# The 71 routed slots of a mixture-of-experts kernel, written out instead of looped over pairs

## The reference, cut to what matters

```python
x = L0_attn_x                                # (4, 1024, 512): 4096 tokens of 512 features
xn = _layernorm(x)
s = _L0_attn_ref(xn, ...)                    # layernorm, q k v, causal softmax, o_proj, + residual
# _L0_ffn_ref, E = 8 experts, K = 2 per token, H = 352:
gates = softmax(xf @ router_w.T)
topv, topi = lax.top_k(gates, K)             # masked gates, divided by their sum
def step(acc, p):
    y = _silu(xf @ wg_e) * (xf @ wu_e) @ wd_e
    return (acc + y * g_e[:, None], None)
routed, _ = lax.scan(step, zeros_like(xf), (wg, wu, wd, masked.T))
shared = _silu(xf @ sg) * (xf @ su) @ sd
g = _silu(routed + shared)
return x + s * g
```

## Time and profile before

| | |
|---|---|
| median of 3 executions | 1150.11 us |
| profiled execution, its own time | 1149.77 us |
| its span, first to last instruction | 1148.0 us |
| PE busy | 1131.4 us (99%) |
| DVE, ACT, POOL busy | 572.4, 473.5, 423.6 us |
| mean granted clock of TensorE | 0.997 of full speed |

### The profile page before, as it was taken

One profiled execution on the slowest core, in us unless ns is written; L12 is line 12 of the kernel. 1 busy time (PEld: TensorE's weight loads), 2 busy tenths in 40 slices (PEclk: granted clock), 3 DMA queues, 4 the chain that ended last, 5 costly groups with the idle time before them and its releaser, 6 DMA issues. The chain is left out here.

```text
span 1148.0 us, 21220 instructions
## 1 busy us (share of the span) xinstructions
PE 1131.4 (99%) x6598; PEld 627.4 (55%) x6599; DVE 572.4 (50%) x1236; ACT 473.5 (41%) x859; POOL 423.6 (37%) x656
## 2 busy tenths in 40 slices
PE   8999999999999999999999999999999999999997
PEld 5555555555556555555555555554454454444454
DVE  6876666677469331222111221112477377367467
ACT  5544344435332232333223232234654645555643
POOL 1333233332400222222222222212755754764763
PEclk9999999999999999999999999999999999999999
DMA  9899999989533599999997777776876777766364
GB/s 277 221 238 215 239 239 224 220 212 239 137 76 67 131 191 206 208 202 203 204 190 197 178 184 175 172 177 152 168 184 171 166 160 189 152 161 184 109 156 120
DMA packets 365003, 209.31 MB, mean 182 GB/s; under 512 B 304308, under 2 KB 314816, under 8 KB 364936
## 3 DMA queue, kind: packets, MB, share of 16 engines
q1 hardware_dynamic: 354104, 172.76, 64.7%
q0 software_dynamic: 10800, 35.69, 12.6%
q10 hardware_dynamic: 32, 0.02, 0.0%
HBM read 89.44 MB, written 46.01 MB: 118 GB/s over the span
## 5 line engine op out<-in xcount | busy, mean ns | idle before, releaser
L706 PE MATMUL pair<-arena 128*128 (+2 forms) x3240 | 506.2, 313 | 2.9 <-DMA arena<-arena 2.7
L706 PEld LDWEIGHTS pair<-arena 128*128 128x128 f16 x3240 | 316.0, 98 | 185.6 <-DMA arena<-arena 3.2
L1647 DVE SCALAR_TENSOR_TENSOR arena<-pair,slot_unit,arena 128x352 f32<-128x352 f32 x71 | 41.5, 584 | 269.1 <-ACT arena L1537 212.6
L713 PE MATMUL bank<-arena 128*128 x639 | 149.3, 379 | 0.0
L1537 ACT ACTIVATE arena<-pair,slot_unit 128x352 f32<-128x352 f32 x71 | 39.3, 554 | 205.4 <-PE pair L706 178.5
L1251 POOL COPY arena<-token_of 128x1 uint32 (+1 forms) x71 | 12.9, 181 | 265.2 <-issue 103.1
L1941 PE MATMUL pair<-arena 128*128 128x512 f16 (+3 forms) x576 | 98.0, 326 | 1.3 <-ACT arena L2009 1.2
L713 PEld LDWEIGHTS bank<-arena 128*128 128x128 f16 x639 | 62.5, 98 | 66.2
L1954 PE MATMUL bank<-arena 128*128 128x512 f16 x411 | 93.5, 379 | 0.0
L1253 POOL DMA_INDIRECT arena<-xn_rows,arena x71 | 71.7, 1010 | 55.6 <-POOL arena L1251 54.0
L1921 PE MATMUL bank<-arena 128*128 128x512 f16 x384 | 86.1, 379 | 0.0
(11 more groups left out here) (205 smaller groups left out, 1360.3 us busy)
## 6 DMA issues: line engine op xcount, KB each, us to landing
slot_rows<-arena SPq DMA_DIRECT2D x71, 256.0 KB
arena<-in_L_attn_x_dram SPq DMA_DIRECT2D x64, 256.0 KB, 3.5
xn_rows<-arena SPq DMA_DIRECT2D x32, 260.0 KB, 2.6
shared_rows<-arena SPq DMA_DIRECT2D x32, 256.0 KB
arena<-shared_rows SPq DMA_DIRECT2D x32, 256.0 KB
out_dram<-arena SPq DMA_DIRECT2D x31, 256.0 KB, 2.8
arena<-in_L_ffn_wg_dram SPq DMA_DIRECT2D x32, 176.0 KB, 3.1
arena<-in_L_ffn_wu_dram SPq DMA_DIRECT2D x32, 176.0 KB, 3.3
```

Of the source, the lines that this page charges most:

```text
L706: last = pe.matmul(bank[:, 0:width], xt[:, a, c, :], weights(c, b, col, width), start=(c == 0 and i == 0), stop=(c == KC - 1 and i == 2))
L713: last = pe.matmul(bank[:, :], ht[:, a, c, :], weights(c, b), start=(start and c == 0 and i == 0), stop=(stop and c == HC - 1 and i == 2))
L1647: v.scalar_tensor_tensor(sbuf[u], u_banks[u][:, 0:H], slot_unit[u][:, 1:2], sbuf[u], ALU.mult, ALU.mult).then_inc(slot_h_ready, 1)
```

## The change

`over_slots` no longer makes a hardware loop. It is a Python loop over all slots from 4 to 70, so that PE, ACT, DVE and POOL get the instructions of every slot one after the other, with a Python number for j, u and k. The waits then compare with constants, the address of `expert_of[j]` and of `token_of[j]` is a constant, and the loop's counter and branch are gone. Order, buffers, semaphores and matmuls are the same.

```diff
             def over_slots(eng, tile, first):
 
-                with eng.Fori(first // 2, (T - 1) // 2) as i:
-                    tile(2 * i, 0, i, False)
-                    tile(2 * i + 1, 1, i, False)
-                tile(T - 1, 0, (T - 1) // 2, True)
+                for j in range(first, T):
+                    tile(j, j % 2, j // 2, j == T - 1)
```

## The result

The kernel with the slots written out takes 1155.60 us, median of 6 executions (1153.04 to 1158.18); the kernel before took 1151.34 us beside it (6 executions). The ratio is 1.0039, 95% interval 1.0025 to 1.0053: slower by 0.4%, where no change was forecast, and 1155.6 us lies above the range's end of 1153.0 us. It is 5.2 us over the forecast of 1150.4; 1.2 of them are the kernel before's own, whose median was 1150.11 us when the forecast was made. The profiled execution of the changed kernel is one of its fastest, 1153.13 us with a span of 1151.4 us, 3.4 us over the span before; it shows the loss at the lower end of its size.

The account below looks back on a forecast made before the run. TensorE's time to stream columns was taken to bound the routed stage. 1149.77 - 0 (loop) + 0.25 (code) = 1150.0 us for the profiled execution, about 1150.4 against the median; range 1148.5 to 1153 us.

Parts of the forecast that it names:

- no change: The forecast itself: TensorE's columns set the routed stage in both forms, 1150.4 us, own range 1149 to 1152, chance 0.86.
- The bound and the loop's price: Routed stage: TensorE's column streaming bounds it at 5.522 us a slot; removing loop counter, branches and register arithmetic gains 0 us.
- the loop costs something after all: Faster rival in the slots: constants remove the sequencer's register work, 1144.6 us; chance 0.05 together with its branch-fetch form.
- a taken branch that fetches its target: Second half of that faster rival: 33 loop branches at 1.2 us each, 40 us, so 1110 us; within the shared 0.05.
- The longer code: Routed stage: some 6200 more TensorE instructions, 25 more q8 packets, 30 us of DMA engine time, 0.25 us of TensorE waiting.
- TensorE is covered against such delays: Slots: transposed rows land 3.4 us after issue with 3.8 us spare, so other engines' code packets cost 0 us.
- A hand-over ... shifted by some 0.1 us may move its own waits by a microsecond: Hand-over from slots to attention: a small shift may move waits by a microsecond; held within the forecast's 1149 to 1152.
- the slower side: Both slower rivals together, slower than the kernel before by more than 2.3 us: chance 0.07 + 0.02 = 0.09.
- starving TensorE: Slower rival in the slots: code packets arrive late for TensorE, 1155 us, or 1180 if all seen; chance 0.07.
- GpSimd's chain: Slower rival: a GpSimd code packet meets a late gather and exceeds the 2.3 us left; 1155 us, chance 0.02.
- 1155: Time given by slower rivals: one in five of 25 packets late by about 1 us, or five GpSimd cases by 1 us.

Follow-up runs that it names:

- e3: ScalarE, VectorE and GpSimd written out, TensorE kept in the loop, against the kernel before: ratio 1.0006 (0.9996 to 1.0017).
- e8: TensorE's slots written out, stores and gathers cut to 64 of 512 columns, against the kernel before: ratio 0.9983, median 1149.36 us.
- e7: Kernel before, still looped, with stores and gathers cut to 64 of 512 columns: ratio to the uncut kernel before 0.9987, median 1149.01 us.
- e5: Only TensorE changed against the kernel before: slots 4 to 37 written out, 38 to 69 in the loop: ratio 1.0035 (1.0019 to 1.0051).
- e6: Only TensorE changed against the kernel before: slots 4 to 37 in the loop, 38 to 70 written out: ratio 0.9992 (0.9979 to 1.0004).
- e10: Changed kernel plus 14 instructions of already satisfied waits at the start of TensorE's program: ratio to the kernel before 1.0006 (0.9996 to 1.0017).
- e11: Changed kernel, SP waiting for the first four slot-output gathers before the attention's first big transpose: ratio to the kernel before 0.9997 (0.9985 to 1.0009).
- e1: The changed kernel itself, timed once more against the kernel before: ratio 1.0059 (1.0045 to 1.0072).
- e14: Kernel before with TensorE's loop starting at slot 6 and SP waiting for four gathers before its first big attention transpose: ratio 1.0005 (0.9995 to 1.0016).
- e4: GpSimd alone written out, the other engines in the loop, against the kernel before: ratio 1.0010 (0.9994 to 1.0026).
- e9: Kernel before, looped, plus 14 instructions of already satisfied waits at the start of TensorE's program: ratio 0.9998 (0.9988 to 1.0008).
- e15: Kernel before, looped, with SP waiting for the first four slot-output gathers before the attention's first big transpose: ratio 0.9998 (0.9987 to 1.0010).
- e13: Kernel before with TensorE's loop starting at slot 6 instead of 4, two more slots written out: ratio 1.0042 (1.0023 to 1.0062).
- e2: TensorE alone written out, the other three engines in the loop, against the kernel before: ratio 1.0035 (1.0020 to 1.0051).

## Why the prediction was wrong, point by point

- *The bound and the loop's price*: right. Slots are 5.53 us apart in both forms, and no gain came from the 33 branches or the register waits. Both halves of the rival "the loop costs something after all" fell, the one by a taken branch that fetches its target too. e3 shows this for the other engines: 1.0006.
- *The longer code*: the count was right, 60 packets on q8 (61 forecast), 24 of them where there was none; 11 on q14 (16 forecast). That TensorE does not starve was right: its matmuls have no idle time without a releaser, and e8 is as fast as e7. The price for the other DMAs was wrong. I counted the packets' own time, 30 us of DMA engine time or 0.5 points of share. The traces show 6.5 points, 65.7% to 72.2% on q1: 0.065 x 16 x 365 = 380 us of DMA engine time, some 16 us for each packet (10 to 12 in e5 and e6, by the same sum); the small packets that start behind a code packet are the slow ones, 67 and 43 ns in the first and second microsecond of the changed kernel's trace against 23. All this time costs the median next to nothing: e10 and e11 have the packets and are at 1.0006 and 0.9997.
- *"TensorE is covered against such delays"*: wrong, by the spare time. I took 3.4 us, the median landing of all transposes of the run, and so 3.8 us spare. A median says nothing on the one that is late, and it was not from this stretch. Issue to last landing of the transposes of gathered rows, worked out one by one for the slots: median 4.2, slowest 6.9 us in the kernel before, with 7.2 available (510.93 - 503.71). The spare time was 0.3 us. With code packets the slowest took 7.2 us in the change's profile, 9.6 in e11's and 10.1 in e1's; in the last two a packet of q8 begins some 6 us behind that issue and takes 2.2 and 2.3 us, and the stage became 6.7 and 4.8 us longer. That the packet did it is not shown. Late transposes happen without one too: 8.0 us in e3, with a packet of q14 on it, and 8.1 in e14, with none of either queue; TensorE waited 0.9 us each time. And single long executions are not the written-out TensorE's alone: e4, with its loop, has one of 1158.66 us in 12. How often it happens can't be said from one profile a run.
- *"A hand-over ... shifted by some 0.1 us may move its own waits by a microsecond"*: this is the step that failed, the term that I left in the own range of "no change". Where SP's transpose starts at +14.2 the gap measures 1.2 to 4.4 us, and the changed kernel's two profiles are 2.7 and 5.9 us longer behind the slots. That the median's loss is in it is shown by taking it away: e10 and e11 put the changed kernel back to 1.0006 and 0.9997. I had read the stretch behind the slots as unchanged because SP's program and TensorE's matmuls are, and reckoned neither with the two issues of 1.88 us by SP, which were in the trace, nor with the transpose 1.1 us behind the gather. A change of TensorE's code length moves every later code packet against the work, and here one of them set how close behind a gather a transpose was issued.
- *The rivals*: the slower side had 0.09 in all, on two mechanisms (starving TensorE, GpSimd's chain) neither of which was at work. The price "1155" was near, by chance. The rule of the Trainium skill ("Runtime: NRT & Kernel Launch", section "Instruction fetch mechanics") that the next block is fetched beside execution agrees with the trace for the engine that runs the code: with 24 packets more its matmuls have no idle time without a releaser. Its remark that kernels prefer full unrolling is not borne out here: unrolled, the kernel is 0.4% slower. The stall that the section gives as the reason, a taken branch to a target outside the window, is not seen in the loop, whose stretch has no packet on q8.

What stays open: by what path a code packet of TensorE holds an issue of SP. That it does rests on the cases: SP's six loads take 0.32 to 0.44 us each, but one of them takes 1.07 to 1.59 in each of the seven kernels in which a packet of q8 begins while SP issues them (the kernel before, e3, e4, e6, e9, e10, e15), and in none of the other ten; and on e10 and e13, which brought a packet there and took it away. Open too is why the gap varies from 1.2 us (e2) to 4.4 (e1) with SP's transpose at the same place.

## What to carry to other kernels

Before code is made longer on the busiest engine, look beyond the stage: the places of all its later code packets move, and two DMAs of different queues that are issued within a microsecond of each other may come closer together or further apart, which here decided whether a gather was usable 5.9 or 11.3 us after its issue; keep them apart with a wait if it matters (e11: 0.9997, where the same kernel without it had 1.0039 and 1.0059). Take spare time from the slowest landing in the stretch, not from a median. A loop of two plain iterations that costs no gap on the bounding engine is worth keeping: nothing is to be had, and the DMA engines are spared the code.

## What the runs showed of the hardware

- A 16 KB code packet in a stretch full of 256-byte packets raises their mean from 23 to 67 or 70 ns for the first microsecond behind it (the change, e2), and costs some 16 us of DMA engine time in all (10 to 12 in e5 and e6).
- A code packet of TensorE came with a longer DMA issue of another engine, 1.07 to 1.59 us instead of 0.43: in seven kernels of seven with a packet at that time, and in none of ten without.
- A gather whose issue had ended before a big transpose was issued was usable 5.9 us after its own issue; one with the transpose 0.16 us behind the start of its issue, after 11.3 us.
- A stall of TensorE of 2.9 us inside the slots, and one of 4.0 us at the hand-over, were each followed by some microseconds at the lower clock level (0.65 and 0.51 of full speed in the stretches above); the stall of 2.1 us in the changed kernel's profile was not.
- A loop body of some 200 instructions on TensorE ran 33 times without one packet on q8 in 365 us.
